# A Trainium2 expert kernel: GpSimd's last two weight splits moved one tile forward, split products from the eighth tile

## What is computed

```python
x = x + xattn(layernorm(x), ctx_512, Wq, Wkv_expand, Wout)
h = layernorm(x)
scores = softmax(h @ gate_weight.T)
topk_w, topk_idx = top_k(scores, 2)
gu  = einsum('th,efh->tef', h, gate_up_weights)
act = silu(gu[..., :352]) * gu[..., 352:]
y   = einsum('tef,te,ehf->th', act, combine, down_weights)
y   = y + shared_expert(h)
x = x + y
```

## Time and profile before

| what | value |
|---|---|
| median of 3 runs | 338.91 us (337.8 to 339.03) |
| the profiled execution | 337.44 us |
| its span | 335.5 us |
| TensorE busy | 322.2 us, 96% of the span |
| VectorE busy | 269.9 us, 80% |
| ScalarE busy | 231.2 us, 69% |
| GpSimd busy | 145.6 us, 43% |
| mean granted clock of TensorE | 0.995 of full speed |

### The profile page before, as it was taken

The page is one execution under the profiler, slowest core; times in us unless marked ns, Lnnn a source line. Parts: engine busy times, 40 slices in busy tenths (PEclk is TensorE's granted clock), DMA queues, the critical chain, the costliest instruction groups (busy, mean ns, idle before and its releaser), DMA issues.

```text
span 335.5 us, 7041 instructions
## 1 busy us (share of the span) xinstructions
PE 322.2 (96%) x2285; PEld 278.7 (83%) x2285; DVE 269.9 (80%) x681; ACT 231.2 (69%) x578; POOL 145.6 (43%) x151
## 2 busy tenths in 40 slices
PE   7999998999999999999999999999999999999990
PEld 6898887777786798989888988899889999999980
DVE  4879999999756278857657998999999999999940
ACT  4666999999845135131235788888899899989830
POOL 3335485887843000343400005678863522432463
PEclk9999999999999999999999999999999999999998
DMA  7999400000004799798699674554645455445244
GB/s 231 381 337 380 151 3 3 3 3 0 3 2 185 266 341 371 295 301 282 225 307 263 186 263 93 124 123 86 116 90 133 87 100 128 111 92 110 53 49 47
DMA packets 32226, 53.03 MB, mean 158 GB/s; under 512 B 7488, under 2 KB 15808, under 8 KB 31168
## 3 DMA queue, kind: packets, MB, share of 16 engines
q1 hardware_dynamic: 24912, 43.31, 38.9%
q0 software_dynamic: 4576, 9.23, 15.6%
q10 hardware_dynamic: 2704, 0.04, 0.6%
HBM read 32.24 MB, written 16.92 MB: 147 GB/s over the span
## 4 chain that ended last, share of the span: by engine, by line
PE 78%; DVE 6%; ACT 6%; DMA 3%; POOL 3%; issue 3%; POOLq 1%; DVEq 0%; ACTq 0%; SPq 0%
PE bank L590 31%; PE bank L916 23%; PE bank L943 5%; PE bank L646 3%; ACT prob L1079 3%; PE bank L947 3%; PE bank L810 2%; PE bank L957 2%; PE bank L953 2%; PE bank L796 2%; PE bank L657 2%; PE bank L582 1%; DVE bn L1320 1%; POOL rstd L460 1%; DMA act_w<-act_e 1%
## 5 line engine op out<-in xcount | busy, mean ns | idle before, releaser
L569 POOL DMA_INDIRECT out<-y_sb,dest x18 | 41.5, 2305 | 89.7 <-ACT y_sb L1256 47.2
L1333 DVE TENSOR_TENSOR gu_parts<-w_gu,gu_parts 128x704 fp32r<-128x704 f32 x84 | 76.1, 941 | 0.6 <-ACT gu_parts L1034 0.6
L1034 ACT ACTIVATE gu_parts<-w_gu 128x704 fp32r x84 | 66.2, 793 | 11.2 <-PE bank L916 10.4
L916 PE MATMUL bank<-gu_parts,xsT_hi 128*128 128x352 f32 x328 | 71.0, 338 | 0.0
L916 PEld LDWEIGHTS bank<-gu_parts,xsT_hi 128*128 128x128 f32 x328 | 54.3, 188 | 5.4 <-issue 4.1
L916 PE MATMUL bank<-gu_parts,xsT_lo 128*128 128x352 f32 x164 | 39.6, 323 | 0.0
L590 PE MATMUL bank<-x2T_hi,w_sg_lo 128*128 128x512 f32 (+1 forms) x88 | 32.6, 371 | 0.1
L590 PE MATMUL bank<-x2T_hi,w_sg_hi 128*128 128x512 f32 (+1 forms) x88 | 32.0, 363 | 0.0
L590 PE MATMUL bank<-x2T_lo,w_sg_hi 128*128 128x512 f32 (+1 forms) x88 | 31.9, 363 | 0.0
L452 POOL TENSOR_TENSOR prob<-prob,rrow 112x448 f32<-112x448 f32 x30 | 27.5, 933 | 8.9 <-DVE rrow L1383 8.9
L530 POOL DMA_INDIRECT xs_dram<-x2n,slot_i x14 | 14.2, 1017 | 36.2 <-DVE eid L1637 32.2
(11 more groups left out here) (219 smaller groups left out, 827.2 us busy)
## 6 DMA issues: line engine op xcount, KB each, us to landing
w_gu<-guT SPq DMA_DIRECT2D x8, 1408.0 KB, 9.5
xs_dram<-no_row SPq DMA_DIRECT2D x1, 5460.0 KB, 19.9
xs_in<-xs_dram SPq DMA_DIRECT2D x21, 256.0 KB, 2.9
w_dn<-dnT SPq DMA_DIRECT2D x8, 512.0 KB, 6.7
act_w<-act_e SPq DMA_DIRECT2D x19, 176.0 KB, 2.1
w_sg<-sguT SPq DMA_DIRECT2D x10, 256.0 KB, 5.4
w_dn<-dnT SPq DMA_DIRECT2D x8, 192.0 KB, 7.5
w_sd<-sdnT SPq DMA_DIRECT2D x5, 256.0 KB, 4.9
```

The lines of the kernel that those rows point to most:

```text
L569: pool.indirect_dma_start(out=out[:, :], out_offset=bass.IndirectOffsetOnAxis(ap=dest[:, i, 0:1], axis=0), in_=y_sb[i % 2][:, :], in_offse ...
L916: ins = pe.matmul(dst[:, 0:F], xsT[x_][:, c, :], gu2[w_][:, c, f0:f0 + F], start=c == 0 and n == 0, stop=c == C - 1 and n == 2)
L1034: act.activation(dst, src, ACT.Copy).then_inc(s[sem], 1)
L1333: dve.tensor_tensor(lo_, src, hi_.bitcast(F32), ALU.subtract).then_inc(s[sem], 1)
```

## The change

The first split down product is down(7) in place of down(9), so TensorE's wait for the seven splits moves from the pass `i == 10` to the pass `i == 8`. GpSimd makes the split of expert `e` behind scatter `e` up to expert 4, that of expert 5 also behind scatter 4, that of expert 6 behind scatter 5 and that of expert 7 behind scatter 6; behind scatter 7 it makes none.

```diff
@@ -72,7 +72,7 @@
-    SPLIT_FROM = 9
+    SPLIT_FROM = 7
     assert SPLIT_FROM * P >= T
@@ -569,8 +569,9 @@
                 pool.indirect_dma_start(
                     out=out[:, :], out_offset=bass.IndirectOffsetOnAxis(ap=dest[:, i, 0:1], axis=0),
                     in_=y_sb[i % 2][:, :], in_offset=None, compute_op=ALU.add).then_inc(s["yst"], 16)
-                if 1 <= i < E:
-                    split_dn_last(i)
+                for e in range(i + (i > E // 2), i + 1 + (i >= E // 2)):
+                    if 1 <= e < E:
+                        split_dn_last(e)
```

## The result

The change makes the kernel slower: 342.28 us against 338.55 us (medians of 4 executions each). The ratio is 1.0108, with a 95% interval from 1.0083 to 1.0133, so +3.7 us (2.8 to 4.5). The forecast was 341.2 us, in a range of 339.5 to 342.9, so the time is in the range. The profiled execution took 342.69 us.

The account below looks back on a forecast made before the run. TensorE was taken to bound the kernel, VectorE close behind. S + 15.35 − 258.17 with S = 245.1, the 0.46 us gain included, gave +2.3 us on the 338.91 us median: 341.2 us, range 339.5 to 342.9.

Parts of the forecast that it names:

- The new wait takes more than the products give: Ahead of down(7), TensorE stands 2 to 3 us for split 7, against 0.46 us gained: +2.3 us net.
- faster: Rival: all seven splits done before down(7), no stall, 0.46 us gained, 338.5 us; chance 0.03.
- short stall: Rival: GpSimd's chain runs tight, split 7 ends 243.0 to 244.5, +0.2 to +1.7 us; chance 0.28 including no effect.
- S: The moment GpSimd's split 7 ends: 245.1 us forecast, bounds 243.0 to 246.9.
- long stall: Rival: doubled splits and VectorE hold each other up, split 7 ends near 246.9 or later, +3.6 to +5 us; chance 0.05.
- The gain of 0.46 us: Tiles 7 and 8 go from plain to split products on TensorE, 0.23 us saved in each.
- The sum from S to the end of down(9): TensorE's work from split 7's end to down(9)'s end: 15.35 us, so the end moves by S − 242.82 us.
- S, by the queue of GpSimd: GpSimd in order: split 5 takes 3.5 us, scatter 6 starts at 240.1, split 7 ends 5.0 us later.
- VectorE beside a split ... up to 0.7 us late: Tiles 4 or 5: VectorE loses 0.64 us per split, TensorE up to 0.7 us late, swallowed by the stall.
- The stall should not cost the clock: Behind down(7)'s wait the clock stays full, costing nothing; if it fell, each microsecond would add up to 0.5 us.

Follow-up runs that it names:

- second profile: The changed kernel timed and profiled once more, no edit: +3.4 us (2.4 to 4.5) over the kernel before.
- the third: The changed kernel timed and profiled a third time, no edit: +3.6 us (2.4 to 4.8) over the kernel before.
- The new order alone: The changed kernel with SPLIT_FROM back at 9, so only GpSimd's order of splits is new: +1.6 us (1.0 to 2.2) over the kernel before.
- The late wait: The changed kernel with TensorE's wait moved from ahead of down(7) to ahead of its third chunk's products: +1.3 us (0.7 to 1.8) over the kernel before.
- The filled wait: The changed kernel with 14 unread transposes of the identity ahead of TensorE's wait: +2.3 us, again +2.6 us, over the kernel before.
- split from tile 8: The kernel before with SPLIT_FROM 8 in place of 9, old order of splits: +2.3 us (1.6 to 3.1) over the kernel before.
- writes of zeros: The kernel before with six GpSimd writes of zeros to split 5's place behind split 4: +0.9 us (0.3 to 1.6) over the kernel before.

## Why the prediction was right, point by point

- **The new wait takes more than the products give.** Right. TensorE waits on line 546 ahead of down(7), 1.7 to 1.8 us in three profiles, where the prediction had 2 to 3, as TensorE itself came later, held up by VectorE. The rivals "faster" and "short stall" are out, and so is the length of the long one: S was 245.4, 245.2 and 245.4. But what the long stall assumed, two engines that hold each other up in turn, is what the rows fit.
- **The gain of 0.46 us.** The sum from S to the end of down(9), which has it, holds to 0.02 us in the second profile and to 0.10 us in the third, so it is there. It was not measured by itself.
- **S, by the queue of GpSimd.** Right to 0.3 us, in part by luck. Split 5 took 3.17 us and not 3.5, which had no effect. Scatter 6 was taken to wait for the landing of scatter 5, 240.1; it started at 241.38 − 0.79 = 240.6, released by the rows of tile 6, which were 1.5 us later than before and not up to 0.7. From there to S it took 4.84 us in place of 5.0. So the wait that set scatter 6 was the wrong one, at nearly the same time.
- **"VectorE beside a split ... up to 0.7 us late".** Too small. The price per split, 0.64 us, was read where a split lay beside gate and up parts only. Beside the second split lies the low part of the down weights, too, which then takes 1.1 us more. The new order alone costs 1.6 us (1.0 to 2.2). It was right that the stall swallows most of this, as S sets the end; what it does not swallow is in S, through the late rows of tile 6. The late wait takes the stall away, and then VectorE's share is nearly all of what is left.
- **"The stall should not cost the clock".** Wrong, and the term that was mis-sized: nothing against 1.57 us in the profiled execution (3.88 − 2.31). It was argued from the 4 us behind the last product, a place where a fall would have had nothing to slow, and which ends just ahead of one (the windows below). In two more profiles with the same idle time the clock held: the chain gives +2.4 to +2.6 us there and +4.35 with the fall. By the mean clocks it fell in at least 5 of 18 executions, which are 1.4 us longer than the others, and in two of the four of the result. The filled wait, at +2.3 and +2.6 us, is what the forecast's +2.3 describes.
- **The range.** It holds the measured time, but its upper part stood for a late split 7 and not for a fall of the clock, nor for the 0.5 us by which the changed kernel's other executions exceed the filled wait's. That the range had room for both is luck. The larger part of the loss, the wait for split 7 with its sum of +2.3 us, was forecast by its mechanism.

The stretch of the earlier trace rows was too short to argue from. The last slice of the clock in the earlier trace rows is an 8, and the windows that follow in the trace before are:

```profile
332.00:333.00 1.00, 0.00 (x0) 0.00 (x0) 0.00 (x0) 0.00 (x0) 0.00 (x0) 0.65 0.95 112
333.00:334.00 1.00, 0.00 (x0) 0.00 (x0) 0.00 (x0) 0.00 (x0) 0.00 (x0) 0.50 0.15 20
```

So that trace has a fall behind idle time, 4.6 us after the last product ended (327.7 us), where the changed kernel's came behind 1.8 us.

What decides in which executions the clock falls stays open: of four profiles with 1.7 to 2.0 us of idle time ahead of a down product, the one that fell does not have the longest.

## What to carry to other kernels

Put a wait right ahead of the first instruction that reads what it waits for: here six products of 1.4 us stood behind a wait that concerned the three after them, and moving it gave back 2.1 to 2.4 us of 3.4 to 3.7. Before work is moved forward on a helper engine, ask what it will lie beside: GpSimd's reads doubled VectorE's down part in the very tile in which VectorE had no room, a cost that stays whether or not anybody waits for GpSimd. And count a stall of TensorE with the clock behind it: here a fall in at least 11 of 30 executions, which were 1.4 to 1.8 us longer. The mean granted clock of every execution shows how often, where one profile shows only itself.

## What the runs showed of the hardware

- TensorE's granted clock fell to the 1.2 GHz level behind an idle time of 1.8 us, from 246.4 to 249.8 us, in one profile. It stayed at 2.4 GHz behind 1.7 us (two profiles of the same program) and behind 2.0 us (split from tile 8). Mean clocks of 0.990 or less are in 11 of the 30 executions of these two programs and in none of 169 others. Behind the last product of the kernel before, it stayed at 2.4 GHz for over 4 us without work and fell at 332.3 us.
- A VectorE subtraction with both inputs in SBUF took 2.32 us beside GpSimd's subtraction, which ended 1.23 us after it was issued, and 1.22 us beside its writes of zeros. The Trainium skill, SBUF — State Buffer, section "Who interferes with whom", has that contention for a GpSimd instruction that reads SBUF and not for one that only writes it; the trace agrees on both sides. That section calls the contention an exclusive lock. The rows above fit that: the subtraction ended about its own 1.2 us after GpSimd's was over, less the 0.1 us by which successive VectorE instructions overlap.
